# Moving the projections of V and of the hosted key to the end of TensorE's attention step, in a one-core decoder layer

## The chip, the cores and the metric

One core of one Trainium2 chip runs the whole program. The metric is the device time in microseconds of one execution; lower is better. The program uses five engines: TensorE (PE), VectorE (DVE), ScalarE (ACT), GpSimd (POOL) and SyncE (SP), which issues the DMAs. Each engine works through its own list of instructions in order and waits on semaphores that the others raise.

## What is computed

The reference is one post-norm decoder layer on x of shape (16, 128, 256): a gated recurrent mixer, a cross attention and a quantised feed-forward net, each followed by a residual and a layer norm. The attention, around which the change lies, is

```
q = (x @ Wq).reshape(b, n, 32, 8)
k, v = jnp.split(ctx @ Wkv, 2, axis=-1)
q = apply_axial_rope(q, pos_map)
k = apply_axial_rope(k, ctx_pos_map)
logits = jnp.einsum('bqhd,bkhd->bhqk', q, k) * scale
w = jax.nn.softmax(logits, axis=-1)
attn = jnp.einsum('bhqk,bkhd->bqhd', w, v)
return attn.reshape(b, n, 256) @ Wout + bout
```

There are 16 batches of 128 rows, 32 heads of width 8, and a context of 128 rows per batch.

## The kernel before, in words

The three layers run one after the other, and neighbouring ones overlap by a few steps. The attention is a software pipeline over the batches: `Pipeline.at(step, s)` calls an engine's `step` with t = s, s-1, ..., s-6, and a function called with `lag` works on batch t = s - lag. So `logitsT(2, 0)` in step s is the first quarter of the transposed logits of batch s-2. Steps 0 to 2 (`BESIDE`) lie among the last steps of the mixer, steps 3 to 15 stand alone, and steps 16 to 21 drain the pipeline. The order inside a step is written out by hand for each engine.

The softmax runs in four quarters (8 heads each). For each quarter PE writes the logits (`logits`, L1062), DVE takes row maxima from PSUM (`rowmax`, L970), and when a batch has all four, PE transposes the maxima (L1073), DVE scales them into `MT` (L979), and SP writes `MT` with four small DMAs into one row of each query tile (`shifts`, L797). Then PE makes the transposed logits, which now have the maximum subtracted (`logitsT`, L1087), ACT takes the exponential (`exp`, L905), and PE multiplies by V (`values`, L1103). There is one pair of PSUM banks for `logitsT`, so a quarter waits for the exponential of the one before.

A context batch gives a V and a K. V of batch s-2 is projected in `projections(2)` (L1047, two matmul instructions) and copied out of PSUM by ACT's `values(2)` (L895). The keys run far ahead of their use: class `Key` hosts key t in any pipeline. Keys 0 to 10 are hosted by the mixer's steps, and keys 11 to 15 by attention steps 3 to 7 (t = 8 + s); the last key that is then still being turned leaves at step 9. One key goes through these places, and the engine of each is named:

- `project` on PE (L740) and `copy` on ACT (L753), in step s
- `rotate` on POOL (L720 to L724), last in POOL's step s
- `cast` on DVE (L769), in step s+1
- `low` on POOL (L778), in step s+2
- `transpose` on SP (L786), last in SP's step s+2

POOL's step is: means(5), the rotation of the queries of batch s (L720 to L724, four instructions as for a key), `key.low`, deviation(5), bias(3), `queries_low(0)` (L845, waits for DVE's L957), `key.rotate`. SP's step is: `shifts(3)`, `queries(1)` (L807), `key.transpose`. SP's `shifts(3)` of step s+1 serves batch s-2, and so the `logitsT(2, 0)` that stands in PE's step s. DVE's step begins with `reciprocal(4)` and `heads(4)`, which read what PE's `sums(3)` (L1116) of the step before wrote, and goes on with `rowmax(2, 3)`.

In step 2 of the attention the mixer's last step follows PE's attention step: eight matmul instructions for the queries (L379), then key 10 (L740).

Of the kernel before, what the change touches and what calls it, by code (L numbers as in the profile page):

```python
# [36 lines left out]
def wait(eng, sem, value):  # L37

    if isinstance(value, int) and value <= 0:
        return  # L40
    eng.wait_ge(sem, value)
# [597 lines left out]
def attention_layer(nc, ctx, res, B, S, D, H, HD):  # L639
# [61 lines left out]
    def col(t):  # L701
        return slice(t, t + 1)
# [182 lines left out]
    def scalar(act):  # L885
        def step(ph, *ts, key=None):
            def values(lag):

                t = ts[lag]
                if t is None:  # L890
                    return
                pairs = V[t % NV].rearrange("p (g e) r -> p g (e r)", e=2).rearrange("p g (e r) -> p g e r", e=4)
                act.wait_ge(kv_done, t + 1)
                wait(act, pv_done, NCH * (t - 1))
                act.activation(pairs[:, :, 0:4:3, 0:HD], psum[:, 5, D:2 * D].rearrange("p (g e d) -> p g e d", e=2, d=HD),  # L895
                               ACT.Copy).then_inc(V_done, 1)

            def exp(lag, c):

                t = ts[lag]  # L900
                if t is None:
                    return
                act.wait_ge(LT_done, NCH * t + c + 1)
                wait(act, pv_done, NCH * t + c - 1)
                act.activation(PB[c % 2], ps_P, ACT.Exp, scale=exp_scale[:, 0:1]).then_inc(exp_done, 1)  # L905

            def sums(lag):

                t = ts[lag]
                if t is None:  # L910
                    return
                act.wait_ge(pv_done, NCH * t + NCH)
                wait(act, poT_done, t)
                act.activation(PO, ps_v, ACT.Copy).then_inc(PO_done, 1)  # L914

            def heads(lag):

                t = ts[lag]
                if t is None:
                    return  # L920
                act.wait_ge(aT_done, t + 1)
                wait(act, y_done, t)
                act.activation(ATT, ps_at, ACT.Copy).then_inc(ATT_done, 1)  # L923

            def variance(lag):

                t = ts[lag]
                if t is None:
                    return
                act.wait_ge(mean_done, t + 1)  # L930
                wait(act, var_done, t)
                act.activation(junk[:], Y[:, t, :], ACT.Square, bias=nmean_r[:, col(t)], scale=D ** -0.5,  # L932
                               accum_out=yvar[:, col(t)]).then_inc(var_done, 1)

            exp(3, 1)
            variance(5)
            exp(3, 2)
            if key is not None:
                key.copy(act)
            values(2)  # L940
            heads(4)
            exp(3, 3)
            sums(3)
            exp(2, 0)
        return step

    def vector(dve):
# [85 lines left out]
    def tensor(pe):  # L1033
        def step(ph, *ts, key=None):
            def projections(lag):

                t = ts[lag]
                if key is not None and key.comes:
                    if t is not None:
                        wait(pe, V_done, t)  # L1040
                    key.project(pe)
                if t is None:
                    return
                wait(pe, V_done, t)
                if t > 2 and (key is None or not key.comes):
                    pe.wait_ge(K_done, B)
                pe.matmul(psum[:, 5, D:2 * D], CT[:, t], WkvS[:, D:2 * D], start=True, stop=True).then_inc(kv_done, 1)  # L1047
# [27 lines left out]
            def logitsT(lag, c):  # L1075

                t = ts[lag]
                if t is None:
                    return
                if c == 0:  # L1080
                    pe.wait_ge(shift_in, 64 * t + 64)
                wait(pe, exp_done, NCH * t + c)
                n, j = slots(c)
                for k in range(4):
                    for b in range(2):
                        rows = slice(R * (j + b), R * (j + b) + R)
                        ins = pe.matmul(ps_P[:, b, k], KT[rows, t, n + k], QT[t % NB][rows, n + k], start=True, stop=True,  # L1087
                                        tile_position=(R * (j + b), 0))
                ins.then_inc(LT_done, 1)
# [18 lines left out]
            def sums(lag):  # L1108

                t = ts[lag]  # L1110
                if t is None:
                    return
                pe.wait_ge(PO_done, t + 1)
                wait(pe, Y_done, t)
                for n in range(NCH):
                    ins = pe.transpose(ps_po[:, n * P:(n + 1) * P], PO[:, n], ident[:])  # L1116
                ins.then_inc(poT_done, 1)
# [20 lines left out]

            logits(2, 3)
            logitsT(3, 1)  # L1140
            projections(2)
            values(3, 0)
            logitsT(3, 2)
            maxima(2)
# [7 lines left out]
            values(3, 3)  # L1152
            logits(1, 2)
            logitsT(2, 0)
            sums(3)
        return step

    def fill_values(pool, i):
# [5 lines left out]
    return dict(sync=sync, gpsimd=gpsimd, scalar=scalar, vector=vector, tensor=tensor, fill_values=fill_values,  # L1164
                fill_keys=fill_keys, fill_queries=fill_queries, filled=filled, Key=Key,
                steps=Pipeline(B, 7, NB, 2), NCH=NCH, V_filled=V_filled, X2_done=X2_done, rq_done=rq_done, MT_done=MT_done, max_done=max_done,
                exp_done=exp_done, V_done=V_done, PO_done=PO_done)


def ffn_weights(nc, ctx, res, w_gate, w_up, w_down, D, I):  # L1170
# [285 lines left out]
def decoder_layer(nc, x, ctx_in, pos, Wi, Wf, Wg, Wo, gnw, Wq, Wkv, Wout, bout, w_gate, w_up, w_down, out):  # L1456
# [6 lines left out]
    with ExitStack() as ctx:  # L1463
        def sb(name, shape, dt=F32):
# [30 lines left out]
        attn = attention_layer(nc, ctx, (X, QS, region_k, region_t, region_a, region_qa, KT, ident, ident16, K, psum,  # L1495
                                         psum16, WkvS, WoutS, boutS, qcos, qsin, kcos, ksin, exp_scale), B, S, D, H, HD)
# [16 lines left out]
        M_KEYS = M_END + 1 + BESIDE - K_FIRST + 1  # L1513
# [10 lines left out]
        with nc.Block() as block:  # L1524
# [156 lines left out]
            @block.tensor  # L1681
            def _(pe):
                mix = mixer["tensor"](pe)
                for s in range(M_END + 1):
                    if s == K_FIRST:
                        tables["transposes"](pe)
                        pe.wait_ge(tables["CT_done"], B // 4)
                    mixer["steps"].at(mix, s, key=mixer_key(s))
                att = attn["tensor"](pe)
                banks = mixer["banks_read"]  # L1690
                pe.wait_ge(banks["i"], NG)
                ffw["total"](pe)
                pe.wait_ge(banks["g"], NG)
                for k in range(BESIDE):
                    mixer["steps"].at(mix, M_END + 1 + k, key=mixer_key(M_END + 1 + k))
                    ffw["transposes"](pe, k)
                    if k == 1:
                        pe.wait_ge(banks["f"], NG)
                        pe.wait_ge(banks["xT"], NG)
                        pe.wait_ge(banks["oT"], NG)  # L1700
                    if k == 2:
                        pe.wait_ge(banks["h"], NG)
                        pe.wait_ge(banks["ni"], NG)
                        pe.wait_ge(tables["v_in"], 8 * 16)
                        pe.wait_ge(ffw["WT_done"], ffw["n_w"])
                        pe.wait_ge(ffw["WT2_done"], ffw["n_w"])
                    attn["steps"].at(att, k)
                mixer["steps"].at(mix, M_END + 1 + BESIDE, key=mixer_key(M_END + 1 + BESIDE))
                pe.wait_ge(banks["x1T"], NG)
                pe.wait_ge(banks["y"], NG)  # L1710
                pe.wait_ge(banks["q"], NG)
                pe.wait_ge(tables["out_in"], 16 * 16)
                for s in range(BESIDE, A_END):
                    attn["steps"].at(att, s, key=attention_key(s))
                feed = ffn["tensor"](pe)
                for s in range(A_END, A_ALL):
                    attn["steps"].at(att, s)
                    f = s - (A_ALL - FEED)
                    if f == 0:
                        pe.wait_ge(attn["MT_done"], B)  # L1720
                    if f == 1:
                        pe.wait_ge(attn["max_done"], NCH * B)
                        pe.wait_ge(attn["exp_done"], NCH * B)
                    if f == 3:
                        pe.wait_ge(attn["V_done"], B)
                    if f >= 0:
                        ffn["steps"].at(feed, f)
                pe.wait_ge(attn["PO_done"], B)
                for s in range(FEED, F_LOOP):
                    ffn["steps"].at(feed, s)  # L1730
                ffn["steps"].loop(pe, feed)
                for s in range(B, F_ALL):
                    ffn["steps"].at(feed, s)
# [25 lines left out]
```

## Time and profile before

| what | value |
|---|---|
| median of 3 runs | 385.05 us (383.14 to 390.17) |
| profiled execution | 384.7 us, span 382.9 us |
| mean granted TensorE clock | 0.886 of full |
| busy: PE, DVE, ACT, POOL | 279.8, 287.0, 238.9, 208.8 us |

The span runs from the first to the last instruction, and 1.8 us of the execution lie around it. Attention steps 3 to 17 fill about 157 to 293 us of the span. Times below are microseconds from the span's start.

### The profile page before, as it was taken

To read this page: it belongs to the slowest core of one execution; us is meant where nothing else is said; L and a number is where in the kernel's file an instruction comes from. 1 tells how busy PE (TensorE), PEld (TensorE's weight loads), DVE (VectorE), ACT (ScalarE), POOL (GpSimd) and SP (SyncE) were. 2 spreads that over 40 slices of the span, in tenths; PEclk is the share of its full clock that TensorE was granted. 3 is DMA by queue.
4 is the path that set the end of the run, shared out by engine and by line. 5 is a ranking of instruction groups with operands and counts; after the bars stand their busy time and mean duration, and the time that the engine had idled before them with its cause. 6 is when DMAs were issued, how large, how long until landed. Compare 5 with 4: busy or idle time off the path is not lost.

```text
span 382.9 us, 9278 instructions
## 1 busy us (share of the span) xinstructions
PE 279.8 (73%) x3172; PEld 183.5 (48%) x3172; DVE 287.0 (75%) x627; ACT 238.9 (62%) x473; POOL 208.8 (55%) x489
## 2 busy tenths in 40 slices
PE   0273555978756474949897999999997486989862
PEld 0142344666544353635564565666664233555541
DVE  2958867999986886355786588888885449999972
ACT  4354198787762222524675477777677538999993
POOL 3303264877879835574878265465411214676673
PEclk9997568899996557867999599999999969999999
DMA  7992000112111121143333222211110000010111
GB/s 200 333 297 35 1 3 0 28 29 46 38 28 27 29 55 29 30 85 30 59 57 58 57 46 43 30 31 33 37 24 3 2 0 3 15 41 29 39 43 55
DMA packets 50744, 19.43 MB, mean 51 GB/s; under 512 B 42000, under 2 KB 49936, under 8 KB 50704
## 3 DMA queue, kind: packets, MB, share of 16 engines
q1 hardware_dynamic: 50704, 18.90, 22.1%
q8 instruction: 24, 0.39, 0.4%
q14 instruction: 16, 0.13, 0.1%
HBM read 8.27 MB, written 2.10 MB: 27 GB/s over the span
## 4 chain that ended last, share of the span: by engine, by line
PE 30%; DVE 15%; POOL 10%; issue 8%; SPq 4%; ACT 4%; DMA 3%; DVEq 1%; POOLq 0%; ACTq 0%
PE psum L1103 7%; PE psum L1062 4%; DVE M L970 4%; PE psum L1087 4%; PE psum L1136 4%; PE psum L1404 3%; SPq L797 3%; DMA qt<-MT 3%; PE psum L1047 2%; PE psum L379 2%; DVE region_q L1379 1%; DVE region_w L1223 1%; SPq L786 1%; ACT region_a L905 1%; POOL rkB L722 1%
## 5 line engine op out<-in xcount | busy, mean ns | idle before, releaser
L970 DVE TENSOR_REDUCE M<-psum 128x8 f32<-128x1024 f32 x64 | 78.2, 1222 | 23.1 <-PE psum L1062 23.0
L905 ACT ACTIVATE region_a<-psum,exp_scale 128x1024 f32<-128x1024 f32 x64 | 71.3, 1115 | 31.5 <-PE psum L1087 31.4
L1103 PE MATMUL psum<-region_a,region_k 128*32 128x128 f32 x1024 | 43.8, 292 | 0.3 <-ACT region_a L905 0.3
L1404 PE MATMUL psum<-FW,FXT 128*128 128x512 f16 x128 | 32.1, 396 | 7.1 <-DVE FXT L1384 5.1
L1062 PE MATMUL psum<-KT,qt 32*128 32x128 f16 x512 | 27.4, 230 | 11.9 <-DVE M L970 10.2
L1087 PE MATMUL psum<-qt,KT 32*128 32x128 f16 x512 | 26.6, 225 | 9.6 <-DMA qt<-MT 7.0
L1103 PEld LDWEIGHTS psum<-region_a,region_k 128*32 128x32 f32 x1024 | 25.4, 113 | 15.3 <-issue 11.3
L1062 PEld LDWEIGHTS psum<-KT,qt 32*128 32x128 f16 x512 | 15.5, 97 | 25.6 <-DVE M L970 16.2
L1087 PEld LDWEIGHTS psum<-qt,KT 32*128 32x128 f16 x512 | 16.0, 97 | 19.4 <-ACT region_a L905 8.7
L1347 ACT ACTIVATE region_q<-psum,gs 128x512 f32<-128x512 f32 x32 | 20.5, 679 | 6.8 <-PE psum L1404 6.7
L914 ACT ACTIVATE region_a<-psum 128x512 f32<-128x512 f32 x16 | 9.6, 597 | 23.4 <-PE psum L1103 23.4
L845 POOL TENSOR_TENSOR region_qa<-RQ,region_qa 128x256 f16<-128x256 f32 x16 | 11.5, 716 | 22.7 <-DVE region_qa L957 22.7
L1404 PEld LDWEIGHTS psum<-FW,FXT 128*128 128x128 f16 x128 | 11.7, 101 | 23.4 <-issue 7.3
L1379 DVE TENSOR_TENSOR region_q<-region_q,psum 128x512 f32<-128x512 f32 x32 | 20.8, 683 | 2.5 <-PE psum L1404 2.1
L379 PE MATMUL psum<-WqS,X1T 128*128 128x256 f32 x64 | 21.0, 485 | 0.3 <-DVE wmean L1213 0.3
L1136 PE MATMUL psum<-WoutS,region_a 128*128 128x256 f32 x64 | 20.0, 439 | 0.5 <-ACT region_a L923 0.5
L1388 DVE TENSOR_REDUCE habs<-region_q 128x1024 f32 (+1 forms) x16 | 19.5, 1217 | 0.4 <-issue 0.3
L1361 ACT ACTIVATE region_q<-region_q,hq 128x1024 f16<-128x1024 f32 x16 | 18.4, 1148 | 1.5 <-POOL hq L1328 1.2
L870 POOL TENSOR_TENSOR t<-y2var,eps 128x1 f32<-128x1 f32 x16 | 3.0, 189 | 29.2 <-ACT junk L932 29.2
L720 POOL TENSOR_TENSOR rkA<-KS,kcos 128x256 f32<-128x256 f32 x16 | 10.4, 653 | 12.8 <-ACT KS L753 12.8
L1422 PE MATMUL psum<-FW,region_g 128*128 128x256 f16 x128 | 16.6, 273 | 0.7 <-DVE X L1392 0.7
L861 POOL TENSOR_TENSOR means<-y2sum,pair 128x2 f32<-128x2 f32 x16 | 3.2, 202 | 24.6 <-DVE X L1007 24.6
(209 smaller groups left out, 788.0 us busy)
## 6 DMA issues: line engine op xcount, KB each, us to landing
X<-in_x_dram SPq DMA_DIRECT2D x4, 512.0 KB, 6.9
out_dram<-X SPq DMA_DIRECT2D x16, 128.0 KB, 1.7
region_k<-in_L_ffn_w_gate_dram SPq DMA_DIRECT2D x1, 1024.0 KB, 11.4
region_k<-in_L_ffn_w_up_dram SPq DMA_DIRECT2D x1, 1024.0 KB, 9.8
region_k<-in_L_ffn_w_down_dram SPq DMA_DIRECT2D x1, 1024.0 KB, 10.7
qt<-MT SPq DMA_DIRECT2D x64, 2.0 KB
region_w<-in_L_attn_Wi_dram SPq DMA_DIRECT2D x1, 256.0 KB, 3.6
region_w<-in_L_attn_Wf_dram SPq DMA_DIRECT2D x1, 256.0 KB, 3.5
```

The lines of the kernel that those rows point to most:

```text
L379: ins = pe.matmul(ps_y[:, k], X1T[:, k, j], WqS[:, j], start=(j == 0), stop=(j == DC - 1))
L905: act.activation(PB[c % 2], ps_P, ACT.Exp, scale=exp_scale[:, 0:1]).then_inc(exp_done, 1)
L970: dve.tensor_reduce(M[:, j:j + 2, n:n + 4], ps_L, AX.X, ALU.max).then_inc(max_done, 1)
L1062: ins = pe.matmul(ps_L[:, b, k], QT[t % NB][rows, n + k], KT[rows, t, n + k], start=True, stop=True, tile_position=(R * (j + b), 0))
L1087: ins = pe.matmul(ps_P[:, b, k], KT[rows, t, n + k], QT[t % NB][rows, n + k], start=True, stop=True, tile_position=(R * (j + b), 0))
L1103: ins = pe.matmul(ps_v[R * g:R * g + R, c], V[t % NV][:, h], PB[c % 2][:, g // 2, 2 * (g % 2) + e], start=(e == 0), stop=(e == 1), tile_po ...
L1136: ins = pe.matmul(ps_y, ATT[:, n], WoutS[:, n], start=(n == 0), stop=(n == DC - 1))
L1347: act.activation(SG[:, half(n)], ps_gate[n], ACT.Silu, scale=gs[:, n, col(t1_)]).then_inc(sg_done[n], 1)
L1361: act.activation(UH[:], HH[:, ph], ACT.Copy, bias=ROUND, scale=hq[:, col(t2)]).then_inc(uh_done, 1)
L1379: dve.tensor_tensor(hh[:, half(n)], SG[:, half(n)], ps_up[n], ALU.mult).then_inc(hh_done[n], 1)
L1388: dve.tensor_reduce(habs[:, col(t1_)], hh, AX.X, ALU.max, apply_absolute_value=True).then_inc(habs_done, 1)
L1404: ins = pe.matmul(psx[n], XT[:, c], w[c][:, half(n)], start=(c == 0), stop=(c == DC - 1))
```

## The change

PE's `projections(2)` moves from the third place in the step to the last but one, behind `logitsT(2, 0)` and ahead of `sums(3)`. ACT's copies of the hosted key and of V move from between `exp(3, 2)` and `heads(4)` to the end of the step, behind `exp(2, 0)`, and V is now copied before the key. Since the key's projection no longer stands ahead of `values(3, 0)` in step 3, a wait for the last of the mixer's key copies is added in front of PE's step 3. POOL's and SP's lists are not touched.

```diff
@@ scalar step @@
             exp(3, 2)
-            if key is not None:
-                key.copy(act)
-            values(2)
             heads(4)
             exp(3, 3)
             sums(3)
             exp(2, 0)
+            values(2)
+            if key is not None:
+                key.copy(act)
@@ tensor step @@
             logitsT(3, 1)
-            projections(2)
             values(3, 0)
...
             logitsT(2, 0)
+            projections(2)
             sums(3)
@@ returned by attention_layer @@
-                exp_done=exp_done, V_done=V_done, PO_done=PO_done)
+                exp_done=exp_done, K_done=K_done, V_done=V_done, PO_done=PO_done)
@@ block.tensor @@
                 pe.wait_ge(tables["out_in"], 16 * 16)
+                pe.wait_ge(attn["K_done"], M_KEYS)
                 for s in range(BESIDE, A_END):
```

## Rows read from the trace of the kernel before

**Rows 1.** The page's chain that ended last, by line.

```profile
PE psum L1103 7%; PE psum L1062 4%; DVE M L970 4%; PE psum L1087 4%; PE psum L1136 4%; PE psum L1404 3%; SPq L797 3%; DMA qt<-MT 3%; PE psum L1047 2%; PE psum L379 2%; DVE region_q L1379 1%; DVE region_w L1223 1%; SPq L786 1%; ACT region_a L905 1%; POOL rkB L722 1%
```

**Rows 2.** Timeline of PE across one late step: start, duration, engine, line, count, idle before.

```profile
244.85 0.39 PE L1087 MATMUL psum<-qt,KT 32*128 32x128 f16 x8
245.40 0.66 PE L1116 MATMUL psum<-ident,region_a 128*128 128x128 f32 x4 [0.17 <-ACT region_a L914]
246.34 0.40 PE L1062 MATMUL psum<-KT,qt 32*128 32x128 f16 x8 [0.28 <-DVE M L970]
246.57 0.38 PE L1087 MATMUL psum<-qt,KT 32*128 32x128 f16 x8
246.88 0.70 PE L1047 MATMUL psum<-WkvS,region_t 128*128 128x256 f32 x2
247.51 0.65 PE L1103 MATMUL psum<-region_a,region_k 128*32 128x128 f32 x16
248.17 0.40 PE L1087 MATMUL psum<-qt,KT 32*128 32x128 f16 x8
```

**Rows 3.** Timeline of ACT in the same step.

```profile
247.00 1.11 ACT L905 ACTIVATE region_a<-psum,exp_scale 128x1024 f32<-128x1024 f32 x1 [0.61 <-PE psum L1087]
```

**Rows 4.** Timeline of ACT in hosted steps 4 and 5.

```profile
175.51 0.38 ACT L753 ACTIVATE KS<-psum 128x256 f32<-128x256 f32 x1
175.77 0.39 ACT L895 ACTIVATE region_k<-psum 128x256 f32<-128x256 f32 x1
...
189.80 1.11 ACT L905 ACTIVATE region_a<-psum,exp_scale 128x1024 f32<-128x1024 f32 x1 [1.19 <-PE psum L1087]
```

**Rows 5.** Timeline of POOL: key 10, then step 4's key, step 5's queries and low part.

```profile
156.94 0.61 POOL L720 TENSOR_TENSOR rkA<-KS,kcos 128x256 f32<-128x256 f32 x1 [6.30 <-ACT KS L753]
...
178.17 0.61 POOL L720 TENSOR_TENSOR rkA<-KS,kcos 128x256 f32<-128x256 f32 x1
...
180.62 0.62 POOL L720 TENSOR_TENSOR rqA<-region_q,qcos 128x256 f32<-128x256 f32 x1
...
182.94 0.67 POOL L778 TENSOR_TENSOR KA<-RK,KA 128x256 f16<-128x256 f32 x1
```

**Rows 6.** Timeline of SP's DMA issues, steps 5 and 7.

```profile
183.63 1.23 SPq L786 DMA_TRANSPOSE KT<-KA  x1
184.91 3.11 SPq L797 DMA_DIRECT2D qt<-MT  x4
...
202.05 2.40 SPq L786 DMA_TRANSPOSE KT<-KA  x1
```

**Rows 7.** Timeline of PE: logitsT(2, 0) of steps 3, 5, 7, 8, 9, and the projections of step 4.

```profile
168.28 0.60 PE L1087 MATMUL psum<-qt,KT 32*128 32x128 f16 x8 [3.29 <-DMA qt<-MT]
...
170.82 1.22 PE L740 MATMUL psum<-WkvS,region_t 128*128 128x256 f32 x2
171.84 1.06 PE L1047 MATMUL psum<-WkvS,region_t 128*128 128x256 f32 x2
...
189.36 0.40 PE L1087 MATMUL psum<-qt,KT 32*128 32x128 f16 x8 [1.08 <-DMA qt<-MT]
...
208.27 0.40 PE L1087 MATMUL psum<-qt,KT 32*128 32x128 f16 x8 [1.98 <-DMA qt<-MT]
...
220.43 0.56 PE L1087 MATMUL psum<-qt,KT 32*128 32x128 f16 x8
...
228.79 0.40 PE L1087 MATMUL psum<-qt,KT 32*128 32x128 f16 x8
```

**Rows 8.** Timeline of PE behind attention step 2: the mixer's query matmuls.

```profile
152.17 3.78 PE L379 MATMUL psum<-WqS,X1T 128*128 128x256 f32 x8
```

**Rows 9.** Busy time by stretch; the number ahead of the DMA share is the granted clock.

```profile
168.30:176.50 8.20, 8.20 (x83) 5.28 (x83) 2.91 (x5) 4.16 (x6) 1.55 (x3) 0.51 0.33 64
176.60:206.20 29.60, 27.36 (x493) 18.09 (x489) 23.64 (x41) 19.92 (x32) 24.39 (x46) 1.00 0.39 57
...
210.30:220.30 10.00, 10.00 (x111) 5.84 (x113) 5.09 (x9) 4.52 (x8) 2.91 (x7) 0.51 0.29 55
```

## Prediction

> **What bounds the kernel now.** I read the chain of waits first, then the timelines of PE, DVE and ACT in one late attention step, then those of POOL and SP in the steps that still host a key.
>
> The chain gives L1047, the projection of V, 2% of the span [rows 1], and it reads as if taking it from its place would give that back. The late steps say otherwise. PE starts logits(2, 3) when DVE's row maximum is done, at 246.34; then come logitsT(3, 1) at 246.57, the projection at 246.88, values(3, 0) at 247.51 and logitsT(3, 2) at 248.17 [rows 2]. The exponential that logitsT(3, 2) must wait for runs from 247.00 to 248.11 [rows 3]. So projection plus values fill, to 0.06 us, a time that PE has to wait through anyway: two paths tie, and to shorten one gives nothing. The end of the step has holes: logitsT(2, 0) starts at 244.85, sums(3) waits to 245.40, and logits(2, 3) waits again to 246.34 [rows 2].
>
> The hosted steps 3 to 7 have another bound, and it is in queues that the diff doesn't touch. Follow key and shift: POOL rotates step 4's key from 178.17, rotates step 5's queries from 180.62, makes the low part at 182.94; SP transposes it at 183.63, and only then, since SP is one queue in order, issues the four shift DMAs at 184.91; their landing releases logitsT(2, 0) of step 5 at 189.36, for which PE idled 1.08 us [rows 5, 6, 7]. The same happened at 168.28 (3.29 us idle) and 208.27 (1.98 us) [rows 7]. So the rotation of one step's key decides when the next step's first exponential can start.
>
> **Late steps, 9 to 17.** Taking the projection out of its place: 0, since the exponential takes over at 248.11 where PE's own work ended at 248.17. Putting it in at the end: behind logitsT(2, 0) at 244.85 come 0.31 us for that group (246.57 to 246.88), 0.63 for the projection (246.88 to 247.51) and about 0.60 for sums (its 0.66 less the tail that overlaps), which ends at 246.39; DVE released logits(2, 3) at 246.34 [rows 2]. So 0.05 us are lost in each of 9 steps, 0.5 us; if the tails overlap less, 0.15 each, 1.4 us; if more, 0. ACT's copy of V, 0.39 us [rows 4], begins when exp(2, 0) ends, and ACT idled 0.61 us there [rows 3], so it is covered; values(3, 0), which now waits for it, has until 248.11. DVE's reciprocal and heads start some 0.35 us later behind the later sums; they stand ahead of rowmax(2, 3), and that has about as much room before PE's maxima. 0 for both.
>
> **Hosted steps: the new loop.** Before, the key was copied early in ACT's step, at 175.51, and POOL took it up at 178.17 without waiting [rows 4, 5]. Now the copy stands behind exp(2, 0), which stands behind logitsT(2, 0), which waits for the shift DMAs, which wait in SP behind the key transpose, which waits for POOL's low part, which stands behind the rotation of the key copied in the step before. That closes a ring once per step:
>
> - logitsT(2, 0) to the end of exp(2, 0): 0.44 + 1.11 = 1.55 us (189.36, 189.80) [rows 4, 7]. The two projections at full clock, 2 x 0.63 behind 0.31, end at 1.57 [rows 2], a tie
> - V copy 0.26 to the key's start, key copy 0.38, release 0.07 (about what 156.94 shows behind its copy): 0.71 [rows 4, 5]
> - key rotation and means: 180.62 - 178.17 = 2.45; query rotation: 182.94 - 180.62 = 2.32; low part to the transpose's issue: 183.63 - 182.94 = 0.69 [rows 5, 6]
> - transpose to the next logitsT(2, 0): 189.36 - 183.63 = 5.73 in one step, 208.27 - 202.05 = 6.22 in another; I take 5.98 [rows 6, 7]
>
> Sum: 1.55 + 0.71 + 2.45 + 2.32 + 0.69 + 5.98 = 13.70 us per hosted step. Nothing else on PE or DVE is that long at full clock: a step without a key takes 228.79 - 220.43 = 8.36 us. In the present kernel steps 5 to 7 take (208.27 - 189.36) / 2 = 9.5 us [rows 7].
>
> **The clock.** After the idle 3.29 us before 168.28 the granted clock stood at 0.51 (1.2 GHz) for the next 8.2 us, and after the 1.98 us before 208.27 it fell to 0.51 for 10 us; after 1.08 us it did not fall: 1.00 from 176.6 to 206.2 [rows 7, 9]. In the ring PE has some 8 us of work in 13.7 and must idle 2 to 5 us before each logitsT(2, 0), so I expect 1.2 GHz in part of each hosted step. At that level the projections sit in the ring: 0.60 for logitsT, 1.02 for the key (170.82 to 171.84), 1.06 for V = 2.68 in place of 1.55 [rows 7], so 14.83 us per step. I take 14.3, midway.
>
> The Trainium skill, "TensorE: Matmul & The Clock Gate", section "HAM oscillation — how this bites in real kernels", describes a loop that waits for a DMA in each turn and starts each turn at half clock. By that rule all five rings would take 14.83 us, which is the third rival below. The trace agrees for idles of 1.98 and 3.29 us and not for 1.08.
>
> **Step 2.** The first V projection leaves a place where PE waited for DVE and goes in front of the eight query matmuls at 152.17, which PE runs back to back for 3.78 us [rows 8] and behind which key 10, its copy and POOL's 156.94 stand [rows 5]. POOL had idled 6.30 us for that copy, so all of it arrives at 168.28 by the same path as above. Cost: 1.06 at 1.2 GHz [rows 7], less if the clock rises as early as before and PE runs the tail faster, in which case 0.6. I take 0.6. The new wait on K_done in front of step 3 delays logits by one copy in a stretch where PE then idles 3.29 us: 0.
>
> **Sum**, against the profiled execution (span 382.9, 384.7 us in all; the median of the runs shown is 0.35 above it):
>
> - logitsT(2, 0) of step 3: 168.28 + 0.6 = 168.9
> - step 4's: one ring at 1.2 GHz without means, 14.83 - 0.15 = 14.68, so 183.6
> - steps 5 to 8: 4 x 14.3 = 57.2, so step 8's at 240.8. Key 15's rotation in step 7 is the last in the ring. Before it stood at 220.43 [rows 7]: +20.4
> - step 8 to 9: before 8.36 us, where 7 to 8, at 1.2 GHz, took 12.16 [rows 7]. The new step 8 comes out of an idle like the old step 7's: +0 to +3.8, I take +2.5
> - late steps: +0.5
>
> 384.7 + 20.4 + 2.5 + 0.5 = 408.1, so 408 us, 6% slower. Low end: four rings at full clock with 5.73 for the DMA part (13.45), no low clock in step 8: 183.3 + 53.8 = 237.1, +16.7, so 401. High end: 1.06 in step 2, all rings 14.83 + 0.24, 3.8 in step 8, 1.4 late: 168.28 + 1.06 + 14.9 + 60.3 = 244.5, +24.1, so 414.
>
> **Rivals.**
>
> *The ring doesn't close.* The keys have slack of many steps (key 11 is used in step 12), and if POOL or SP had room to run ahead, the late copy would cost nothing. Then only 0.5 late and 0.6 in step 2 remain, and 386 us. For it: keys really aren't needed soon. Against it: SP holds the shifts behind the transpose in the rows above, and its list isn't changed.
>
> *Faster.* If the tie at 248.11 is not real (an exponential that starts earlier once PE is free sooner), each of 9 late steps could give up its 0.63 us, and the two projections of the hosted steps likewise, if POOL's late rotation is absorbed as in the first rival: 384.7 - 9 x 0.63 = 379 us. It decides as soon as logitsT(3, 1) moves forward; but DVE's maximum, which releases logits(2, 3) at 246.34, stands in front of both [rows 2], so I give it little.
>
> *1.2 GHz throughout.* PE is slow in all rings and its own body grows towards the ring: PE's step from 208.27 to 220.43 took 12.16 us, mostly at 0.51 and without a key [rows 7, 9]; with a key at 1.02 and DVE waiting for the late queries it can reach 15 us and more. Five at 15.3: 168.9 + 76.5 = 245.4, +25.0, with 3.8 and 0.5 behind it 414 us, up to 417.
>
> **Chances.** Forecast 0.78, ring doesn't close 0.08, faster 0.04, 1.2 GHz throughout 0.10. I give 400 to 415: the forecast's bounds and part of the third rival. A measurement of this kernel can tell about 2% (7.7 us) from no change. Faster 0.04, same 0.08, slower 0.88.
>
> **What would show it.** In the profile after: POOL's key rotation (L720 on KS) in steps 3 to 7 idles until ACT's L753, several us each; SP's L786 is issued late and L797 right behind it; PE idles 2 us or more for the shift DMA before L1087 five times; distances between those are 13.5 to 15 us; the clock is at 0.5 in part of 170 to 250 us; a late step grows by 0.05 to 0.15 us. If the hosted steps keep to 10 us, the ring was misread. If they are longer but PE idles at L970 or L1103 and not at the DMA, the bound is elsewhere.

## The result, and the profile after

The changed kernel takes 405.54 us in the median of 4 runs (402.17 to 408.15), the kernel before 386.45 us beside it (383.14 to 390.17). The ratio is 1.0538, with a 95% interval of 1.0472 to 1.0603: 5.4% slower. (Some executions run in a slower state and are left out of the ratios, so a ratio is not the quotient of the two medians.) The forecast was 408 us, 400 to 415. The profiled execution took 408.0 us, its span is 406.2 us against 382.9 before.

The first row to read is that of POOL's groups in the page. Before, the rotation of a key stood idle 12.8 us over the whole span for its copy; now this is one of the largest waits of the page:

```profile
L720 POOL TENSOR_TENSOR rkA<-KS,kcos 128x256 f32<-128x256 f32 x16 | 10.5, 656 | 45.2 <-ACT KS L753 45.2
L1087 PE MATMUL psum<-qt,KT 32*128 32x128 f16 x512 | 28.4, 237 | 25.7 <-DMA qt<-MT 14.1
```

The same two waits in the table of waits of the changed kernel, for 165 to 250 us (total, times, longest):

```profile
POOL rkA L720 <- ACT KS L753: 32.3, 5, 7.4
...
PE psum L1087 <- DMA qt<-MT: 13.3, 5, 4.2
```

Five rotations wait for five late copies. PE waits five times for the shift DMAs as well, but the first of these waits (2.34 us) stands ahead of step 3, and of the five turns of the ring behind it three end with a long wait, one with 0.60 us and one with next to none, as PE's timeline below shows. The chain of waits of the changed kernel, from step 5's logitsT(2, 0) to step 6's, goes once round the ring that the prediction drew, on the branch through PE's projections (start, duration, what):

```profile
198.46 0.61 PE psum L1087 x8
199.07 1.15 PE psum L740 x2
200.22 0.87 PE psum L1047 x2
...
201.39 0.39 ACT KS L753
...
201.85 0.61 POOL rkA L720
...
204.42 0.57 POOL rqA L720
...
206.74 0.64 POOL KA L778
207.40 1.26 SPq L786
...
208.71 0.66 SPq L797
...
210.77 1.69 DMA qt<-MT
...
212.51 0.61 PE psum L1087 x8
```

POOL rotates the key, then the next queries, then makes the low part; SP transposes, then issues the shifts. It answers to [rows 5, 6], where the rotation had started at 178.17 without waiting. PE's timeline gives the length of each turn. These are logitsT(2, 0) of steps 3 to 9, which answer to [rows 7]:

```profile
169.28 0.61 PE L1087 MATMUL psum<-qt,KT 32*128 32x128 f16 x8 [2.34 <-DMA qt<-MT]
...
183.94 0.40 PE L1087 MATMUL psum<-qt,KT 32*128 32x128 f16 x8 [3.22 <-DMA qt<-MT]
...
198.46 0.61 PE L1087 MATMUL psum<-qt,KT 32*128 32x128 f16 x8 [4.17 <-DMA qt<-MT]
...
212.51 0.61 PE L1087 MATMUL psum<-qt,KT 32*128 32x128 f16 x8 [2.94 <-DMA qt<-MT]
...
226.48 0.40 PE L1087 MATMUL psum<-qt,KT 32*128 32x128 f16 x8
...
239.29 0.61 PE L1087 MATMUL psum<-qt,KT 32*128 32x128 f16 x8 [0.60 <-DMA qt<-MT]
...
252.43 0.63 PE L1087 MATMUL psum<-qt,KT 32*128 32x128 f16 x8
```

The five turns took 14.66, 14.52, 14.05, 13.97 and 12.81 us, 70.0 in all, where the kernel before took 220.43 - 168.28 = 52.15 [rows 7]: +17.9 us. Step 8 to 9 took 13.14 us against 8.36: +4.8. The granted clock of these stretches answers to [rows 9]:

```profile
199.00:201.50 2.50, 2.50 (x9) 2.03 (x8) 0.00 (x0) 1.50 (x3) 0.00 (x0) 0.50 0.36 66
212.60:225.00 12.40, 12.20 (x119) 7.83 (x119) 5.80 (x9) 5.88 (x9) 7.62 (x14) 0.50 0.23 45
...
239.40:252.00 12.60, 12.40 (x133) 7.74 (x131) 6.28 (x11) 5.61 (x8) 3.81 (x9) 0.50 0.34 64
```

Here 0.50 is 1.2 GHz. The late steps did not change. PE's timeline of one of them, to be held against [rows 2]:

```profile
276.82 0.39 PE L1087 MATMUL psum<-qt,KT 32*128 32x128 f16 x8
277.13 0.70 PE L1047 MATMUL psum<-WkvS,region_t 128*128 128x256 f32 x2
277.67 0.60 PE L1116 MATMUL psum<-ident,region_a 128*128 128x128 f32 x4
278.30 0.40 PE L1062 MATMUL psum<-KT,qt 32*128 32x128 f16 x8
278.54 0.39 PE L1087 MATMUL psum<-qt,KT 32*128 32x128 f16 x8
278.85 0.65 PE L1103 MATMUL psum<-region_a,region_k 128*32 128x128 f32 x16
280.13 0.40 PE L1087 MATMUL psum<-qt,KT 32*128 32x128 f16 x8 [0.64 <-ACT region_a L905]
```

The projection and sums(3) now fill the two holes at the end of the step, and a hole of 0.64 us stands where the projection was, in front of logitsT(3, 2), which waits for the exponential. From one logitsT(2, 0) to the next it is 284.90 - 276.82 = 8.08 us; before, 252.93 - 244.85 = 8.08 us.

### The profile page after: what moved, and what is told of

Same layout as the page of the kernel before. It is cut to its first block, busy times and chain, and to the rows that moved or that the text cites. A ratio compares the mean times of both kernels' runs of the same rounds, so it can differ in the third digit from the quotient of the medians.

```text
span 406.2 us, 9279 instructions
## 1 busy us (share of the span) xinstructions
PE 287.3 (71%) x3172; PEld 192.2 (47%) x3172; DVE 292.0 (72%) x627; ACT 240.0 (59%) x473; POOL 210.9 (52%) x489
## 4 chain that ended last, share of the span: by engine, by line
PE 29%; POOL 13%; DVE 10%; issue 8%; ACT 6%; SPq 6%; DMA 3%; DVEq 1%; POOLq 0%; ACTq 0%
PE psum L1103 4%; SPq L797 4%; PE psum L1087 4%; PE psum L1062 4%; DMA qt<-MT 3%; PE psum L1136 3%; ACT region_a L905 3%; PE psum L379 3%; PE psum L1047 3%; PE psum L1404 2%; SPq L786 2%; DVE region_q L1379 1%; PE psum L740 1%; POOL rkB L721 1%; POOL RQ L724 1%
## 5 line engine op out<-in xcount | busy, mean ns | idle before, releaser
L1087 PE MATMUL psum<-qt,KT 32*128 32x128 f16 x512 | 28.4, 237 | 25.7 <-DMA qt<-MT 14.1
L1103 PE MATMUL psum<-region_a,region_k 128*32 128x128 f32 x1024 | 46.2, 304 | 0.3 <-ACT region_a L905 0.3
L1404 PE MATMUL psum<-FW,FXT 128*128 128x512 f16 x128 | 31.2, 387 | 7.4 <-DVE FXT L1384 5.4
L1062 PE MATMUL psum<-KT,qt 32*128 32x128 f16 x512 | 28.5, 237 | 10.4 <-DVE M L970 7.8
L1087 PEld LDWEIGHTS psum<-qt,KT 32*128 32x128 f16 x512 | 17.3, 102 | 36.3 <-ACT region_a L905 19.6
L1103 PEld LDWEIGHTS psum<-region_a,region_k 128*32 128x32 f32 x1024 | 26.7, 118 | 12.7 <-issue 7.8
L1062 PEld LDWEIGHTS psum<-KT,qt 32*128 32x128 f16 x512 | 16.2, 100 | 25.1 <-DVE M L970 13.7
L988 DVE RECIPROCAL rs<-psum 128x32 f32<-128x32 f32 x16 | 5.7, 358 | 24.8 <-PE psum L1116 24.3
L1136 PE MATMUL psum<-WoutS,region_a 128*128 128x256 f32 x64 | 21.9, 472 | 0.5 <-ACT region_a L923 0.5
L379 PEld LDWEIGHTS psum<-WqS,X1T 128*128 128x128 f32 x64 | 15.6, 255 | 3.3 <-DVE wmean L1213 0.3
```

The lines of the kernel that those rows point to most:

```text
L379: ins = pe.matmul(ps_y[:, k], X1T[:, k, j], WqS[:, j], start=(j == 0), stop=(j == DC - 1))
L1062: ins = pe.matmul(ps_L[:, b, k], QT[t % NB][rows, n + k], KT[rows, t, n + k], start=True, stop=True, tile_position=(R * (j + b), 0))
L1103: ins = pe.matmul(ps_v[R * g:R * g + R, c], V[t % NV][:, h], PB[c % 2][:, g // 2, 2 * (g % 2) + e], start=(e == 0), stop=(e == 1), tile_po ...
L1136: ins = pe.matmul(ps_y, ATT[:, n], WoutS[:, n], start=(n == 0), stop=(n == DC - 1))
L1404: ins = pe.matmul(psx[n], XT[:, c], w[c][:, half(n)], start=(c == 0), stop=(c == DC - 1))
```

## The experiments

"SP's shifts" below are the first of the four small DMAs of each step. The distance between two of them is a hosted step, and five such steps ("five turns") lie between those that release step 3's logitsT(2, 0) and those that release step 8's. They take 213.35 - 163.56 = 49.8 us in the kernel before and 235.52 - 165.51 = 70.0 in the changed one. These lengths come from one execution of each kernel.

**V alone.** The key's projection and copy go back to their old places.

```diff
@@ scalar step @@
             exp(3, 2)
+            if key is not None:
+                key.copy(act)
...
@@ tensor step @@
             logitsT(3, 1)
+            key_projection(2)      # the key's part of projections(2)
             values(3, 0)
```

> Only V moves: its projection and its copy stand at the end of the step, the hosted key's stay where they were. Ring theory (the key's late copy delays POOL's rotation, that SP's key transpose, that the shift DMAs, once per hosted step): the ring isn't there, so 385 to 388 us; steps 3 to 8 take some 52 us from the first logitsT(2, 0) to the last, as before the change, where they took 70 with it; the late steps grow by 0.05 to 0.15 us. Rival (a projection at the end of PE's step costs by itself, through the later sums and maxima): 393 us or more.

Measured: 385.25 us, ratio to the kernel before 0.9979 (0.9931 to 1.0028), five turns 50.6 us (166.30 to 216.89). The late steps stayed at 8.07 us (233.02 to 241.09), where I had expected 0.05 to 0.15 more. V's move costs nothing that can be told and gives nothing, so the loss isn't in what stands at the end of PE's step as such.

**The key alone.** V goes back; the key's projection and copy stay at the end. (V's projection then waits for the key copy of the step before, which uses the same PSUM bank.)

> Only the key moves: its projection and copy stand at the end of the step, V's stay where they were. Ring theory: all of the loss stays, 401 to 406 us, and the hosted steps take 13 to 15 us each. Rival (the loss is in V's projection, or in the two together on PE): 393 us or less.

Measured: 402.61 us, ratio 1.0468 (1.036 to 1.0575), five turns 65.5 us (163.86 to 229.34), of 12.5 to 13.7 us each where I had expected 13 to 15. POOL's timeline has its rotations idle again:

```profile
182.92 0.61 POOL L720 TENSOR_TENSOR rkA<-KS,kcos 128x256 f32<-128x256 f32 x1 [5.26 <-ACT KS L753]
...
196.84 0.61 POOL L720 TENSOR_TENSOR rkA<-KS,kcos 128x256 f32<-128x256 f32 x1 [6.10 <-ACT KS L753]
```

The loss goes with the key. Its turns are 0.9 us shorter than with both; V's projection no longer stands in the ring, which would account for that. This reading of the 0.9 us is an argument, not a test of its own, and it sets the shortest of this kernel's executions (399.94 us) against one of the longer of the changed kernel's (408.01).

**The ring cut at SP.** The changed kernel, with the key transposes a step later, behind the shifts. Nothing else moves.

```diff
             shifts(3)
+            if key is not None:
+                key.transpose(sp)
             queries(1)
-            if key is not None:
-                key.transpose(sp)
...
-                attention_key(BESIDE).transpose(sp)
...
-                    attn["steps"].at(step, s, key=attention_key(s))
+                    attn["steps"].at(step, s, key=attention_key(s - 1) if s > BESIDE else None)
```

> The changed kernel with one thing more: SP issues a key's transpose one step later, behind that step's shift DMAs. POOL, ACT, PE and DVE keep their order, the key is copied as late as in the changed kernel. Ring theory: the shifts no longer wait for POOL, so a hosted step falls from 14 to 9 or 10 us (now DVE's wait for the rotated queries sets it), TensorE's clock stays up, and the whole takes 380 to 388 us. Rival (the late copy costs on ACT, or the late projections on PE): 400 us or more.

Measured: 382.11 us, ratio 0.9885 (0.9775 to 0.9995). With the late copy still there and POOL still waiting for it (16.9 us in five waits, against 32.3), the kernel is back at the time of the kernel before. Three of its turns in SP's timeline:

```profile
173.33 2.67 SPq L797 DMA_DIRECT2D qt<-MT  x4
176.05 2.18 SPq L786 DMA_TRANSPOSE KT<-KA  x1
...
182.67 2.67 SPq L797 DMA_DIRECT2D qt<-MT  x4
185.79 1.53 SPq L786 DMA_TRANSPOSE KT<-KA  x1
...
196.56 2.71 SPq L797 DMA_DIRECT2D qt<-MT  x4
199.32 1.24 SPq L786 DMA_TRANSPOSE KT<-KA  x1
...
205.85 2.68 SPq L797 DMA_DIRECT2D qt<-MT  x4
```

The shifts now come ahead of the transpose, 9.3 us apart in two of these three turns. The turn of 13.9 us fell together with a low clock (0.54 over 184 to 192 us), so the clock did not stay up as I had expected. All five turns took 53.9 us (161.76 to 215.62), 4.1 more than in the kernel before; the shifts had begun 1.8 us earlier, and the turn behind took 9.1 us where the kernel before took 11.7, so that both issue the shifts for step 10's logitsT(2, 0) at 232.8 to 233.0 us.

The kernel before with this same order in SP, which is tried further down, gains as well (0.9775). Held against that one, the move still costs about 1.1%, and the two intervals overlap: of 5.4% some four fifths went with SP's order. For the rest the chain of waits of this run shows a second, shorter ring without SP: key copy, both rotations on POOL, casts and a row maximum on DVE, PE's logits and projections, and the next key copy (key rotation at 203.13, row maximum at 209.25, key projection at 211.05, next rotation at 212.89, a turn of 9.76 us). No run cuts this one.

**The ring cut at POOL.** The changed kernel, with the low part of key t-1 made ahead of the rotation of key t.

```diff
             queries(0)
-            if key is not None:
-                key.low(pool)
+            if key is not None and key.first:    # key 9, in step 3
+                key.low(pool)
...
             queries_low(0)
             if key is not None:
+                key.low(pool, ahead=True)        # key t-1
                 key.rotate(pool)
```

> The changed kernel, with POOL making the low part of the key before ahead of the rotation that waits for the late copy, and not behind the next queries. SP's order is as in the changed kernel. Ring theory: the transpose no longer waits for the rotation, 380 to 388 us, hosted steps of 9 to 10 us. Rival (SP's transposes and shifts are slow by themselves, or PE's late projections): 400 us or more.

Measured: 390.22 us, ratio 1.0137 (1.0037 to 1.0236), five turns 48.5 us (164.19 to 212.69). The hosted steps are as short as the theory said. But the median is 2 us above the range I gave, and about 1.4% of the loss is still there; the runs go from 385.1 to 392.8 us, and the ratio rests on the two lowest. The profiled execution is the lowest of the four. In it the next turn took 12.8 us, at a clock of 0.50 over 216 to 224 us, but the same turn took 11.7 us in the kernel before, so this hardly explains the other runs. They have no trace, and what keeps them up is open.

**The clock.** The changed kernel with matmuls that nobody needs where PE waits for the shifts.

```diff
             logits(1, 2)
+            if ts[0] is not None and 3 <= ts[0] <= 8:
+                for _ in range(24):
+                    pe.matmul(psum[:, 4, 256:384], ident16[:], ident16[:], start=True, stop=True)
             logitsT(2, 0)
```

> The changed kernel with 24 idle 128x128 matmuls (into an unused part of PSUM) ahead of logitsT(2, 0) in steps 3 to 8, where PE waits for the shift DMAs. They keep TensorE busy and release nothing. If the low clock lengthens the hosted steps by 1.1 us each and the step behind them by nearly 4: clock at 1.00 from 170 to 250 us and 394 to 400 us. If the ring is bound by POOL and SP alone and the clock is only a companion: 403 to 407 us, the clock up all the same.

Measured: 400.44 us, ratio 1.0376 (1.0309 to 1.0443), so about 5 us less than the changed kernel and just outside the range I gave for the clock. The clock did not come up to 1.00 throughout: it is 0.93, with a low stretch between 208 and 224 us. PE in one such step, and both kernels over 170 to 240 us, the filled one first (the clock is the number ahead of the DMA share):

```profile
190.79 1.51 PE L1155 MATMUL psum<-ident 128*128 128x128 f16 x24
194.44 0.40 PE L1087 MATMUL psum<-qt,KT 32*128 32x128 f16 x8 [2.13 <-DMA qt<-MT]
```

```profile
170.00:240.00 70.00, 55.12 (x934) 38.55 (x934) 43.50 (x65) 35.38 (x55) 41.72 (x76) 0.93 0.23 44
```

```profile
170.00:240.00 70.00, 53.81 (x716) 35.34 (x717) 38.60 (x58) 31.82 (x49) 39.47 (x72) 0.77 0.24 40
```

Five turns took 66.9 us (163.41 to 230.26), and the last four 13.3 each on average. The two of them that ran wholly at 1.00 took 12.8 and 13.5 us, so that is the ring at full clock, and the DMA wait stays in it. So of the 19 us lost, the fill gave back some 5, which belong to the clock; some 14 stay, most of them the ring itself. As the clock was not up all the time, its share may be a little more.

**A longer rotation.** Two more products on POOL, 0.57 us each, in the rotation of each of keys 11 to 15, in the changed kernel and in the kernel before.

```diff
+        for spare in extra:        # two spare tiles for keys 11 to 15
+            nc.gpsimd.tensor_tensor(heads_of(spare[:]), heads_of(x), c, ALU.mult)
         nc.gpsimd.tensor_tensor(heads_of(a[:]), heads_of(x), c, ALU.mult)
```

> The changed kernel with two more of POOL's 0.57 us products in the rotation of each of the five keys 11 to 15, written to spare tiles that nobody reads. Ring theory: the rotation is on the ring once a step, so all of 5 x 1.14 = 5.7 us arrives, 411 us. Rival (POOL has room, it waits over 5 us for each key copy): no change, 405 us.

> The kernel before with the same two products more in each of the five rotations. There the chain passes through one rotation in every second step, so 2 to 3 of them count: +1 to +3 us, 387 to 390 us; POOL has no idle time ahead of the rotation there. If it came out at +5.7, the loop before would be as tight as the new one.

Measured: 412.29 us, ratio 1.0676 (1.0605 to 1.0747), in the changed kernel; 389.30 us, ratio 1.0071 (1.0003 to 1.0139), in the kernel before. The first is 1.3 us above the 411 that I expected, the second inside its range. 5.7 us of added work show as 1.4% or 5 us in the first (7 us by the medians), where five turns grow from 70.0 to 76.2 (164.43 to 240.60) and the chain of waits goes through all five lengthened rotations. So POOL stands idle 5.6 to 7.5 us ahead of every rotation, and yet what the rotation takes is paid in full.

In the second it shows as 0.7% or 3 us, and the chain of waits goes through two of the five rotations, as forecast. But the five turns of its profiled execution grew by 6.1 us too, to 55.9 (163.23 to 219.13). What goes beyond two rotations (2.3 us) fell together with a lower clock, 0.69 over 192 to 200 and 0.50 over 216 to 224 us, where the kernel before had 1.00 and 0.70; 1.7 us came back in the turn behind. With their intervals the two costs, 1.4% and 0.7%, can't be told apart. So this pair shows that the rotation is on the path of the changed kernel; that it weighs less in the old one rests on the chain and not on the times.

**SP's order with the key early.** If the queue is what binds, the kernel before has something to gain as well. Two kernels, the first of them run twice: V at the end, key early, transposes behind the shifts; and the kernel before with SP's order alone.

> V at the end of the step as in the change, the hosted key where it was before, and SP's key transposes one step later, behind the shifts. Ring theory: neither the late copy nor the transpose stands before the shifts, hosted steps of 8.5 to 9.5 us, and TensorE hardly waits for the DMAs: 376 to 381 us. If SP's order was of use only against the late copy: 385 us, as with V alone.

> The kernel before, with SP's key transposes one step later and nothing else. If the whole gain of V at the end plus the new SP order is SP's order: 374 to 377 us. If V's place gives part of it (it shortens what PE has between two exponentials in the hosted steps, where two projections stood): 377 to 381 us. Late steps at 8.08 us either way.

> The kernel with V at the end and SP's key transposes one step later, run again beside the one without V's move: 373 to 377 us. The difference to that one is what V's place is worth once SP's queue is out of the way.

Measured: V at the end with SP's order 374.78 us, ratio 0.9703 (0.9642 to 0.9763), and when run again 377.68 us, 0.9820 (0.9768 to 0.9872); SP's order alone 375.84 us, 0.9775 (0.9716 to 0.9835). All three beat the kernel before by some 2 to 3% (that it is 2% or more is clear in the first alone) and the changed kernel by 7 to 8%. The first lies 1 us below the range I gave and the second 0.7 above it; V's place makes no difference that can be told. SP's timeline of the kernel with SP's order alone:

```profile
182.31 2.67 SPq L797 DMA_DIRECT2D qt<-MT  x4
185.42 1.25 SPq L786 DMA_TRANSPOSE KT<-KA  x1
...
190.82 2.71 SPq L797 DMA_DIRECT2D qt<-MT  x4
...
199.25 2.68 SPq L797 DMA_DIRECT2D qt<-MT  x4
...
207.33 2.68 SPq L797 DMA_DIRECT2D qt<-MT  x4
```

From 173.88 us on its hosted steps take 8.1 to 8.5 us, hardly longer than a late step, and with V at the end 8.1 us from the third on, shorter than the 8.5 to 9.5 I had expected. In the kernel before, steps 5 to 7 took 9.5 on average [rows 7].

The Trainium skill, "DMA: Bandwidth & Descriptors", section "Issuing engines are not separate DMA queues", says that issuing from several engines saves only the sequencer's time to start a DMA, usually small beside the DMA itself. No run here issues from a second engine. In SP's queue a shift took 0.64 us to issue and a transpose mostly 1.23 (up to 2.40 in the kernel before), and the four shifts with 2.68 us took longer than the 1.69 from the last issue to the landing, so here that time is not small beside the DMA. But what was worth 10 us in the kernel before (385.90 to 375.84), and 23 in the changed one (405.54 to 382.11), was what the queue waited for in between.

## Why the prediction was right

**The ring.** Forecast as logitsT(2, 0), exp(2, 0) or the two projections in a tie, key copy, key rotation, query rotation, low part, transpose, shifts, once per hosted step. The chain after shows these in this order in all five turns, each time through the projections and not through exp(2, 0), also where the turn began at full clock. Cutting it at SP brought the kernel back to its old time (four fifths of the loss, against the old kernel with the same order in SP), cutting it at POOL took most of the loss away, moving V alone did not bring it, moving the key alone brought nearly all of it, and lengthening one member lengthened the whole. The rival that the ring doesn't close and the one that the kernel gets faster are out.

**Its length.** Forecast 14.7 for the first turn and 14.3 for the others, 71.9 in all; measured 70.0. At full clock I had worked out 13.70, and the filled kernel shows 12.8 and 13.5. The member that I made too large is transpose to logitsT: I took 5.98 from two rows, and the five turns after took 5.93, 6.34, 5.11, 5.05 and 5.05. The part up to the rotation was right: at 1.2 GHz the rotation starts 201.85 - 198.46 = 3.39 us into the turn, as forecast.

**The clock.** It fell in part of the hosted steps, as forecast, and filling the waits gave 5 us back. The third rival, 1.2 GHz throughout with turns of 15.3 us, didn't come: two of the turns began at full clock (logitsT at 183.94 and 226.48 took 0.40 us, at the other three 0.61). But it came near. Where the clock was low from 212.6 to 225.0, PE's own work ended at 226.36 and the DMA landed for 226.48; in the turn behind PE waited 0.60 us. So my sign that PE idles 2 us or more for the shift DMA in each turn held in three of the five (3.22, 4.17 and 2.94 us).

**Step 8 to 9.** Forecast +2.5 out of 0 to 3.8, measured +4.8: outside the bounds. I took the old step 7 to 8 (12.16 us) as the worst case, but that one began at full clock, and the new one ran at 0.50 from end to end.

**Step 2.** Forecast +0.6. From step 2's first logits (145.34 before, 146.69 after, a difference that stands ahead of every moved instruction) to POOL's rotation of key 10 it is 11.60 before and 12.19 after: +0.59. It was given back at once, since the next shift DMAs took 3.77 us from first issue to landing (165.51 to 169.28) and not 4.72 (163.56 to 168.28, from the timelines). I had let it pass in full.

**Late steps.** Forecast 0.05 us each, 0.5 in all; measured 0. The term off is the projection's length at its new place: 277.67 - 277.13 = 0.54 us in front of transposes, against 0.63 in front of values. logits(2, 3) starts at 278.30, no later than DVE allows. That taking it out gives nothing was right, for the reason given: the exponential takes over.

The sum by the trace: +1.00 up to step 3's logitsT (of which 1.35 stand ahead of the change, and the rest gives 0.35 back), +17.86 in the five turns, +4.78 behind them, and the rest of the span 0.34 us shorter: 23.3, which is 406.2 - 382.9.

**Luck in the number.** That the profiled execution took 408.0 us where I had said 408 is partly luck. The five turns were 1.9 us shorter than forecast and the late steps 0.5, step 8 to 9 was 2.3 longer and step 3's logitsT 0.4 later, and these cancel. The 408.0 is also one of the longer two of the four runs: the medians differ by 19.1 us, 4 less than the two profiled executions.

## What to carry to other kernels

Before you move a producer to the end of a step, follow its consumers through every queue, and not only to the place where the data is used: the key had nine steps of slack, and the queues that carried it had none. In SP's queue an issue that waited for its data held all that stood behind it (transpose at 207.40, shifts at 208.71), so put the ones whose data is ready earlier first. Here this one swap is worth 2% in a kernel where all engines look busy, and with it the late key costs about 1% and not 5%. Filling an engine's holes gives nothing when the engine is not what the step waits for: PE's holes moved, and the step stayed 8.08 us.

## What the runs showed of the hardware

The clock can stay at its low level while PE is nearly always busy: 0.50 from 239.4 to 252.0 us with 12.40 of 12.60 us busy (windows above), as it had been at 0.51 with 10.00 of 10.00 us busy in the kernel before [rows 9]. New is what stood ahead of it. From 228.85 to 231.8 the clock was 1.00; PE then had waits for exponentials of 0.64 us ahead of 230.14 and 1.10 us ahead of 232.97, and from there it was low:

```profile
232.50:239.00 6.50, 5.72 (x60) 3.40 (x60) 3.20 (x7) 2.40 (x4) 5.16 (x11) 0.51 0.22 42
```

The rows before had shown it low only behind single idles of 1.98 and 3.29 us, and not behind 1.08 [rows 7, 9]; so a wait of 1.1 us can be followed by either level.

The first cast of DVE takes about twice as long when it starts together with POOL's low part. In the changed kernel L957 took 0.88 us at 191.49, 0.08 us after POOL had begun one, and 0.42 at 247.16, when POOL was idle:

```profile
191.49 0.88 DVE L957 CAST region_qa<-RQ 128x512 f16<-128x512 f32 x1 [0.18 <-POOL RQ L724]
...
247.16 0.42 DVE L957 CAST region_qa<-RQ 128x512 f16<-128x512 f32 x1
```

Between 140 and 310 us all six casts that met a low part's start took 0.88 us, in the kernel before (161.66) and in the changed one; one that met only a low part's last 0.2 us took 0.46 (221.23), and all 21 beside an idle POOL took 0.42. It was not varied in an experiment.

The part from a key's transpose to the landing of the four shift DMAs varied between 5.05 and 6.34 us with the same work. What makes the difference was not tried.
